# The first 14 slots of a GRU and attention-gated GRU kernel get an order of their own on every engine

## What is computed

```python
def step(h, xp):                       # first recurrence, 50 steps
    hp = h @ Ur + b[1]
    z = sigmoid(xz + hz); r = sigmoid(xr + hr)
    hc = tanh(xh + r * hh)
    return z * h + (1.0 - z) * hc
emb = concatenate([hs, news_b - hs, news_b, hs * news_b], axis=-1)
a = relu(emb @ att_W1 + att_b1); a = relu(a @ att_W2 + att_b2)
ats = sigmoid(a @ att_W3 + att_b3)
def au_step(h, xs):                    # second recurrence, on the first one's states
    u = sigmoid(xu_t + h @ au_Uu); r = sigmoid(xr_t + h @ au_Ur)
    c = tanh(xc_t + r * (h @ au_Uc))
    u_ = at_t * u
    return (1.0 - u_) * h + u_ * c
x = batch_norm(concatenate([h_final, news])); x = leaky(x @ d_W1 + d_b1); x = leaky(x @ d_W2 + d_b2)
y = sigmoid(x @ f_W + f_b)
```

## Time and profile before

| what | value |
|---|---|
| median of 3 runs | 1980.85 us (1979.35 to 1981.06) |
| profiled execution | 1982.23 us, span 1980.4 us |
| PE busy in the span | 1937.3 us, 98% |
| start to R(4) | 36.34 us |
| R(4) to R(14) | 89.20 us |
| R(14) to R(196) | 1737.73 us |
| R(196) to the end | 117 us |

### The profile page before, as it was taken

How to read it: one execution, slowest core, us unless ns; L and a number is a source line. 1 busy time by engine, 2 the same in 40 slices (tenths; PEclk the granted TensorE clock), 3 DMA queues, 4 the chain that set the end, 5 groups by cost and what they waited for, 6 DMA issues and landing times.

```text
span 1980.4 us, 29691 instructions
## 1 busy us (share of the span) xinstructions
PE 1937.3 (98%) x9180; PEld 860.6 (43%) x9180; DVE 1499.0 (76%) x2356; ACT 1452.0 (73%) x2464; POOL 1642.1 (83%) x1396
## 2 busy tenths in 40 slices
PE   6799999999999999999999999999999999999998
PEld 2244444444444444444444444444444444444443
DVE  6677777777777777777777777777777777777775
ACT  5577777777777777777777777777777777777764
POOL 5688888888888888888888888888888888888862
PEclk9899999999999999999999999999999999999999
DMA  3111111111111111111111111111211111111110
GB/s 105 48 54 49 70 50 51 48 69 48 50 70 50 48 64 53 52 49 69 48 48 69 53 48 51 66 48 53 69 48 48 69 48 53 48 69 48 38 44 22
DMA packets 37146, 108.15 MB, mean 55 GB/s; under 512 B 4282, under 2 KB 4538, under 8 KB 30594
## 3 DMA queue, kind: packets, MB, share of 16 engines
q1 hardware_dynamic: 37122, 107.86, 15.4%
HBM read 107.43 MB, written 0.42 MB: 54 GB/s over the span
## 4 chain that ended last, share of the span: by engine, by line
PE 92%; POOL 3%; DVE 2%; issue 1%; ACT 1%; DMA 1%; SPq 0%; DVEq 0%; POOLq 0%; ACTq 0%
PE ps L762 29%; PE ps L763 29%; PE ps L764 29%; PE ps L825 3%; PE ps L816 1%; POOL hn_lo L282 1%; POOL h_lo L288 1%; POOL d L331 1%; DMA score<-score_rows 0%; POOL gus L321 0%; ACT hn_hi L372 0%; DMA x<-in_xs 0%; POOL g_lo L312 0%; POOL x_lo L335 0%; DVE ps L570 0%
## 5 line engine op out<-in xcount | busy, mean ns | idle before, releaser
L762 PE MATMUL ps<-h_hi,w_hi 128*128 128x512 f16 x1384 | 526.5, 380 | 16.2 <-DVE a_lo L650 5.9
L763 PE MATMUL ps<-h_lo,w_hi 128*128 128x512 f16 x1384 | 525.7, 380 | 0.0
L764 PE MATMUL ps<-h_hi,w_lo 128*128 128x512 f16 x1384 | 525.4, 380 | 0.0
L282 POOL TENSOR_TENSOR hn_lo<-hn,hn_hi 128x512 f16<-128x512 f32 x200 | 232.9, 1164 | 187.1 <-ACT hn_hi L372 187.1
L276 POOL TENSOR_TENSOR hn<-h,news 128x512 f32<-128x512 f32 x200 | 256.0, 1280 | 86.5 <-DVE h L668 78.6
L446 ACT ACTIVATE ps<-gt,p_rest 128x512 f32<-128x512 f32 x196 | 135.3, 690 | 216.8 <-DVE gt L665 216.8
L321 POOL TENSOR_TENSOR gus<-gu,score 128x512 f32<-128x512 f32 x200 | 254.8, 1274 | 5.4 <-DMA score<-score_rows 3.8
L331 POOL TENSOR_TENSOR d<-h,hc 128x512 f32<-128x512 f32 x196 | 249.9, 1275 | 6.0 <-ACT hc L474 6.0
L762 PE MATMUL ps<-x_hi,w_hi 128*128 128x512 f16 x599 | 229.3, 383 | 14.4 <-POOL x_lo L335 5.1
L312 POOL TENSOR_TENSOR g_lo<-g,g_hi 128x512 f16<-128x512 f32 x196 | 228.1, 1164 | 17.6 <-ACT g_hi L478 17.6
L656 DVE TENSOR_TENSOR gt<-gr,ps 128x512 f32<-128x512 f32 x196 | 134.9, 688 | 140.3 <-ACT gr L481 140.3
(11 more groups left out here) (123 smaller groups left out, 3706.1 us busy)
## 6 DMA issues: line engine op xcount, KB each, us to landing
x<-in_xs SPq DMA_DIRECT2D x200, 256.0 KB, 3.1
score<-score_rows SPq DMA_DIRECT2D x50, 1024.0 KB, 4.7
news<-in_xs SPq DMA_DIRECT2D x1, 1024.0 KB, 8.5
score_rows<-s_rows SPq DMA_DIRECT2D x50, 8.0 KB
p_rest<-in_pack_rest SPq DMA_DIRECT2D x1, 776.0 KB, 9.3
p_att<-in_pack_att SPq DMA_DIRECT2D x1, 322.0 KB, 6.4
p_gru<-in_pack_gru SPq DMA_DIRECT2D x1, 195.0 KB, 2.6
p_state<-in_pack_state SPq DMA_DIRECT2D x1, 192.0 KB, 8.5
```

Source lines behind the costliest of these rows:

```text
L282: g.tensor_tensor(hn_lo[:, k, :], hn[:, k, :], hn_hi[:, k, :], ALU.subtract).then_inc(hnlo_ready, 1)
L762: m.matmul(ps[:, bank, :], w_hi[:, w, :], hi, start=start, stop=False)
L763: m.matmul(ps[:, bank, :], w_hi[:, w, :], lo, start=False, stop=False)
L764: return m.matmul(ps[:, bank, :], w_lo[:, w, :], hi, start=False, stop=stop)
```

## The change

Slots 4 to 13 get a function `early` of their own on PE, ACT, DVE and POOL, and `slot` is left with slots from EARLY = 14 on. In detail:

- Step 0: R has two banks (B_R and B_A2), so R of item 1 needs no wait and R of item c waits for ACT's r of c - 2. DVE makes t in one instruction. ACT computes 1 - z directly (scale -1 and the bias negated, `b_keep`), so that h is one multiplication. ACT takes the r of item 0 before the fourth x_hi, and DVE two t and one h before the attention weights are prepared.
- Loads: x of item 0 is started from ACT's own queue, ahead of everything on ACT; the state's weights come before the attention's; the candidate news in four parts, `p_rest` after x of step 1.
- Weight splits: state on POOL (after the x_lo of step 0), attention on DVE, gated weights in halves, the hi part on ACT and the lo part on DVE, in slots 8 and 12.
- Slots 4 to 13: the candidate hc goes to PSUM (bank B_GHH, not yet in use), and d = h - hc is made by DVE, not POOL, in place of which e and h take d in place. `attention_1` writes alternately B_GXH and B_A1 for items below 8. The first scores come in slot 8 instead of 9. GXH comes before Z instead of after it.
- Ten matmuls on a zeroed tile come first on PE (`WARM`); their result is not used.
- The batch norm's small instructions go to DVE's slots 196 to 199.

The diff, cut to what the text speaks of:

```diff
-B_Z0, B_XH0 = (B_Z, B_GHH), (B_XH, B_HH)
-B_NEWS = (B_GXH, B_A2, B_GXH, B_XH)
+B_R0, B_Z0, B_XH0 = (B_R, B_A2), (B_Z, B_GHH), (B_XH, B_HH)
+B_NEWS = (B_GXH, B_A1, B_XH, B_A2)
+B_HC = B_GHH
...
+    FIRST_SCORED = SCORED - 1
+    EARLY = LAG + NC
     LOW_DVE = 2
-    AHEAD = 2
+    WARM = 10
+    SPLIT_X, SPLIT_G = LAG - 2, LAG + 2
...
             sp.dma_start(p_gru[:, :], pack_gru).then_inc(gru_landed, 16)
-            for c in range(NC):
-                load_x(0, c).then_inc(x_landed[c], 16)
+            load_x(0, 1).then_inc(x_landed[1], 16)
+            load_x(0, 2).then_inc(x_landed[2], 16)
+            load_x(0, 3).then_inc(x_landed[3], 16)
+            sp.dma_start(p_state[:, :], pack_state).then_inc(state_landed, 16)
             sp.dma_start(p_att[:, :], pack_att).then_inc(att_landed, 16)
-            sp.dma_start(news[:, :, :], xs[T, :, :].rearrange("p (c n) -> p c n", c=NC)).then_inc(news_landed, 16)
-            sp.dma_start(p_state[:, :], pack_state).then_inc(state_landed, 16)
-            sp.dma_start(p_rest[:, :], pack_rest).then_inc(rest_landed, 16)
+            load_news(0)
+            load_news(1)
...
+            g.memset(hn_hi[:, 0, :], 0.0).then_inc(warm, 1)
...
+            def split_state():
+
+                hi = w_hi[:, U_Z:U_Z + 3, :].rearrange("p k m -> p (k m)")
+                lo = w_lo[:, U_Z:U_Z + 3, :].rearrange("p k m -> p (k m)")
+                pool.wait_ge(state_landed, 16)
+                g.tensor_copy(hi, p_state[:, :]).then_inc(state_half, 1)
+                pool.wait_ge(state_half, 1)
+                g.tensor_tensor(lo, p_state[:, :], hi, ALU.subtract).then_inc(state_split, 1)
+
+            def early(low):
+                if low + 2 >= NC:
+                    input_low(low + 2, low + 3)
+                if has(low - LAG - 1):
+                    gated_share(low - LAG - 1, low - LAG, NC)
+                if has(low - 1):
+                    state_news(low - 1, low)
+                    state_low(low - 1, low)
+                    state_news_low(low - 1, low)
+
...
+            a.dma_start(x32[:, 0, :], xs[0, :, 0:CH]).then_inc(x_landed[0], 16)
...
+            first_high(0)
+            first_high(1)
+            first_high(2)
+            act.wait_ge(b_ready, 2)
             reset_first(0)
-            candidate_first(0)
+            first_high(3)
             update_first(0)
             reset_first(1)
-            state_high(0, 1)
+            candidate_first(0)
+            update_first(1)
             reset_first(2)
             candidate_first(1)
+            state_high(0, 1)
+            update_first(2)
+            reset_first(3)
+            candidate_first(2)
+            second_high(0)
             state_news_high(0, 1)
-            update_first(1)
+            state_high(1, 2)
+            update_first(3)
+            candidate_first(3)
             act.wait_ge(att_landed, 16)
             news_part(0)
-            reset_first(3)
-            candidate_first(2)
-            update_first(2)
-            state_high(1, 2)
+            state_high(2, 3)
             state_news_high(1, 2)
             news_part(1)
+            second_high(1)
             relu_1_high(0, 1)
-            candidate_first(3)
-            update_first(3)
             news_part(2)
+            act.wait_ge(a1_pe, 1)
+            state_news_high(2, 3)
+            second_high(2)
...
+                act.wait_ge(t2_ready, low + 1)
+                a.activation(ps[:, B_HC, :], t[:, low % 2, :], ACT.Tanh, bias=b_h).then_inc(hc_ready, 1)
+                act.wait_ge(z_pe, low + 1)
+                a.activation(ps[:, B_Z, :], ps[:, B_Z, :], ACT.Sigmoid, bias=b_zr[:, 0:1]).then_inc(z_ready, 1)
+                if low == NC:
+                    relu_1_high(2, 3)
+                if has(low - LAG - 3):
+                    act.wait_ge(g_ready, low - LAG - 2)
+                    a.activation(g_hi[:, (low - LAG - 3) % NC, :], g32[:, (low - LAG - 3) % NC, :], ACT.Copy).then_inc(ghi_ready, 1)
+                input_high(low + 3, 16 * ((low + 3) // NC + 1), low)
+                if low == SPLIT_X:
+                    split_gated_high(0)
+                if low == SPLIT_G:
+                    split_gated_high(1)
...
-                v.tensor_scalar(t[:, c % 2, :], r[:, c % 2, :], b_hs, None, ALU.mult).then_inc(t1_ready, 1)
-                dve.wait_ge(t1_ready, c + 1)
                 dve.wait_ge(xh_pe, c + 1)
-                v.tensor_tensor(t[:, c % 2, :], t[:, c % 2, :], ps[:, B_XH0[c % 2], :], ALU.add).then_inc(t2_ready, 1)
+                v.scalar_tensor_tensor(out=t[:, c % 2, :], in0=r[:, c % 2, :], scalar=b_hs, in1=ps[:, B_XH0[c % 2], :],
+                                       op0=ALU.mult, op1=ALU.add).then_inc(t2_ready, 1)
 
             def new_state_first(c):
 
                 dve.wait_ge(hc_ready, c + 1)
                 dve.wait_ge(z_ready, c + 1)
-                v.tensor_tensor(ps[:, B_Z0[c % 2], :], hc[:, c % 2, :], ps[:, B_Z0[c % 2], :], ALU.mult).then_inc(e_ready, 1)
-                dve.wait_ge(e_ready, c + 1)
-                v.tensor_tensor(h32[:, c, :], hc[:, c % 2, :], ps[:, B_Z0[c % 2], :], ALU.subtract).then_inc(h_ready, 1)
+                v.tensor_tensor(h32[:, c, :], hc[:, c % 2, :], ps[:, B_Z0[c % 2], :], ALU.mult).then_inc(h_ready, 1)
...
+            def early(low):
+                k = low % 2
+                if pairs_of(low - 1):
+                    low_2(0, paired(low - 1))
+                dve.wait_ge(hh_pe, low - NC + 1)
+                dve.wait_ge(r_ready, low + 1)
+                v.scalar_tensor_tensor(out=t[:, k, :], in0=ps[:, B_HH, :], scalar=b_hs,
+                                       in1=r[:, k, :], op0=ALU.add, op1=ALU.mult).then_inc(t1_ready, NC + 1 if low == NC else 1)
+                if has(low - LAG - 1):
+                    gated_difference(low - LAG - 1, low - LAG)
+                dve.wait_ge(c_ready, min(low - 1, NC))
+                item = low - 2 if low > NC else 1
+                attention_1_news(item, item + 1)
+                if pairs_of(low - 1):
+                    low_2(1, paired(low - 1))
+                dve.wait_ge(t1_ready, low + 1)
+                dve.wait_ge(xh_pe, low + 1)
+                v.tensor_tensor(t[:, k, :], t[:, k, :], ps[:, B_XH, :], ALU.add).then_inc(t2_ready, 1)
+                if has(low - LAG - 1):
+                    gated_step(low - LAG - 1, low - LAG)
+                attention_1_low(item, item + 1)
+                if has(low - LAG - 1):
+                    gated_state(low - LAG - 1, low - LAG)
+                dve.wait_ge(hc_ready, low + 1)
+                v.tensor_tensor(d[:, k, :], h32[:, low % NC, :], ps[:, B_HC, :], ALU.subtract).then_inc(d_early, 1)
+                dve.wait_ge(d_early, low - NC + 1)
+                dve.wait_ge(z_ready, low + 1)
+                v.tensor_tensor(d[:, k, :], d[:, k, :], ps[:, B_Z, :], ALU.mult).then_inc(e_ready, NC + 1 if low == NC else 1)
+                dve.wait_ge(e_ready, low + 1)
+                v.tensor_tensor(h32[:, low % NC, :], d[:, k, :], ps[:, B_HC, :], ALU.add).then_inc(h_ready, 1)
+                if low == NC:
+                    dve.wait_ge(c_ready, 3)
+                    attention_1_news(2, 3)
+                    attention_1_low(2, 3)
+                if low == SPLIT_X:
+                    split_gated_low(0)
+                if low == SPLIT_G:
+                    split_gated_low(1)
...
+                if s == LOOP_HI:
+                    dve.wait_ge(rest_landed, 16)
+                    bn_guess()
+                    bn_newton(0)
+                if s == LOOP_HI + 1:
+                    bn_newton(1)
+                    bn_newton(2)
+                if s == LOOP_HI + 2:
+                    bn_newton(3)
+                    bn_fold()
+                if s == LOOP_HI + 3:
+                    bn_news()
...
+            pe.wait_ge(warm, 1)
+            for _ in range(WARM):
+                m.matmul(ps[:, B_A1, :], hn_hi[:, 0, 0:P], hn_hi[:, 0, :], start=True, stop=True)
...
+                    if c >= 2:
+                        pe.wait_ge(r_ready, c - 1)
+                    split_product(B_R0[c % 2], W_R, *x, start=True, stop=True).then_inc(r_pe, 1)
...
+                news_part(c)
+            pe.wait_ge(att_split, 1)
+            pe.wait_ge(c_ready, 1)
+            attention_1(0, 1)
+            pe.wait_ge(state_split, 1)
+            pe.wait_ge(t2_ready, NC)
+            candidate_state(0, 1)
...
+            def early(low):
+                x = (x_hi[:, low % NC, :], x_lo[:, low % NC, :])
+                h = (h_hi[:, (low - NC) % HIST, :], h_lo[:, (low - NC) % HIST, :])
+                hg = (h_hi[:, (low - LAG) % HIST, :], h_lo[:, (low - LAG) % HIST, :])
+
+                pe.wait_ge(r_ready, low)
+                if score_of(low - 1):
+                    pe.wait_ge(s_ready, scored(low - 1))
+                pe.wait_ge(xlo_ready, low + 1)
+                split_product(B_R, W_R, *x, start=True, stop=False)
```

(49 more changed lines are left out.)

354 lines of the change are left out of this document (192 added, 162 removed).

## The result

The changed kernel takes 1973.73 us (median of 7 runs, 1971.77 to 1976.53), the kernel before 1980.85 (7 runs, 1979.35 to 1982.16): ratio 0.9964, 95% interval 0.9952 to 0.9975. It is faster by 7 us where 19 were forecast, and at 1973.73 us it lies 1.7 us above the range of 8 in 10 (1950 to 1972). Its profiled execution took 1972.17 us with a span of 1970.3.

What follows compares the result with a forecast made beforehand. PE bounds the kernel, busy 98% of the span; R(14) to R(196) stays 1737.73 us. A gain of 21.8 us ahead of R(14), less 3 at the end, makes -18.8: 1962.0 us, 8-in-10 range 1950 to 1972.

Steps and rivals of the forecast that it cites:

- Start to R(4): Kernel start to first matmul of slot 4's R product: 36.3 us becomes 23.4.
- the two held instructions: In step 0, two waits where DVE and POOL hold each other up, charged 2.4 us.
- The warm-up's gift: Ten warm-up matmuls cost nothing; what they give the first products is hidden by ACT's r.
- R(4) to R(6): Slots 4 and 5, between starts of their R products: 16.8 us becomes 15.0.
- POOL now sets the pace: Up to R(6), each item costs POOL four instructions, 4.6 us; hn_lo of item 3 ends at 33.8.
- R(6) to R(10): Slots 6 to 9: 36.4 us becomes 24.0, PE setting the pace at 5.2 us a slot, with d on DVE.
- rival 3: Slots 6 to 9: POOL stays pacemaker at 7.5 us a slot (+9), time 1972; 1968 to 1976, chance 0.19.
- R(9)'s wait: Slot 9's R product waits 1.6 us for the score's sigmoid, behind other work on ACT.
- R(11) to R(14): Slots 11 to 13: GXH ahead of Z waits 2.8 us for g; 18.6 us to R(13), then 13.2.
- The clock, +3: Slots 11 to 13: clock falls behind two of three waits, 1.5 us each; between 0 and 6.
- The end, +3: After R(196): batch norm in slots 196 to 199 costs 3.5 us a slot, less slack; 3 of 0 to 7.
- rival 2: Slots 196-199: all 27 batch-norm instructions wait for POOL, 28.0 us, time 1987; 0.06 with anything beyond 1977, half at full price.

Runs made afterwards that it cites:

- run 3: Changed kernel with one DVE instruction moved: c_news of item 2 in slot 4 ahead of a_lo of item 1; 1973.0 us, ratio 0.9955.
- run 10: Two kernels: changed kernel without its ten warm-up matmuls, 1977.23 us; changed kernel with first input again on SP's queue behind p_gru, 1976.09 us.
- run 7: Changed kernel with GXH behind Z (slots 11-13), c_news of item 2 earlier, 22 small batch-norm instructions singly in slots 14-35, large one in 196; 1957.88 us.
- run 9: Changed kernel with d = h - candidate on POOL again in slots 4 to 13 and the candidate in SBUF; 1982.09 us, ratio 1.0007.
- run 1: Changed kernel with the GXH product of slots 11 to 13 behind Z again; 1967.85 us, ratio 0.994.
- run 2: Changed kernel with ten useless matmuls on PE ahead of the wait for g in slots 11 to 13; 1972.38 us, ratio 0.9958.
- e_spread: Changed kernel with GXH behind Z, c_news of item 2 earlier, batch norm spread over step 0 and slots 14, 196, 198, 200; 1965.41 us, ratio 0.9917.
- e_bn_late: Changed kernel with its batch-norm instructions moved from slots 196-199 to slots 200 and 201; 1973.51 us, ratio 0.9969.
- run 5: Changed kernel with the batch-norm instructions back in early slots, where the kernel before has them; 1981.67 us, ratio 1.0.

## Why the prediction was right or wrong

The span was to be 1961.6 and is 1970.3. The 8.7 us are 5.9 ahead of R(14) and 2.9 in the end; the median lies another 1.6 above the profiled execution.

**Start to R(4), 23.4 against 24.27: right in the number**, with errors in it that cancel. r of item 0 starts at 7.26 for 8.2 and h of item 0 at 10.52 for 12.1; the two held instructions cost 1.9 us for the 2.4 charged. Without a fall of the clock step 0 is 22.8 (run 3); the fall costs 1.5. The warm-up's gift was put at nothing, as hidden by ACT's r; it is 2 us (run 10). R(4) also matters less than the sum takes it to: R(6) doesn't follow it (run 3).

**R(4) to R(6), 15.0 against 18.89: the step that failed.** I had "POOL now sets the pace" and ran its instructions back to back to R(6). They are so up to hn_lo of item 3, which starts at 31.48 us. Then POOL stood 3.64 us for x_hi(7), behind an ACT that stood for a DVE instruction placed behind h. I had walked the queue of one engine and not the other two. In place of POOL's pace PE had two waits that the sum lacks, 1.88 us for t and 2.06 for a_lo(3), and about 1.2 us of a fall. Run 3 moves the instruction: the wait for t goes, the other falls to 1.6, and R(6) is at 39.8. The last 1.5 us to the forecast 38.4 stay also in run 7; there too POOL stands for x_hi(7), 1.25 us, and PE 1.63 us for a_lo(3).

**R(6) to R(10), 24.0 against 26.09: PE sets the pace, as forecast.** Slots 6 and 7 take 5.67 and 5.18 us, and rival 3 had 7.5. That the time itself falls in rival 3's interval, 1968 to 1976, is chance. But the reason that I gave, d on DVE, isn't what makes these two slots 5.2: run 9 has d on POOL, and the same slots but for a fall in slot 6. Mis-sized is R(9)'s wait, 2.66 for 1.6; z, x_hi and the gated split stand ahead of the sigmoid on ACT, as I had written, and take longer than I counted. The rest is the tail of a clock fall in slot 6 (0.5 us) and odd parts.

**R(11) to R(14): right.** The wait for g was put at 2.8 and is 2.93, 2.94 and 3.25; 9.58 and 13.16 us against 9.3 and 13.2. I took it as the price of the change and did not say that it could be left out. It could: run 1.

**The clock, +3: near in its sum, by luck.** Up to R(14) this execution shows three falls, at 17 to 22, 40.9 to 44 and 92.4 to 95.3 us, of 1.5 to 1.8 each. I charged two behind the waits for g, and these had one of the three. The first is ahead of R(4) and doesn't reach R(6), so 3.2 us count. What a fall costs was right (1.5). Run 2 ties the falls in slots 11 to 13 to PE's idle time.

**The end, +3 against +5.9: mechanism right, size off.** Two held instructions to a series, 3.4 to 3.6 us against 3.5 priced. The mis-sized term is the slack that was to take them in, 0.5 to 1.5 us a slot. The first series costs nothing (R(197) is on time), the second 1.4, the third 0.9, and the rest appears behind R(199): 3.6. The slack was counted anew for each slot, and the lateness adds up instead. A likely reason, which no run isolates, is that DVE idles where it waits for ACT and POOL, and these are late for the same reason. I also miscounted: 22 small instructions, not 26, which leaves the price of a series as it is and rival 2 too dear. Rival 2 is refuted, as POOL does run dry.

The rule of the Trainium skill ("SBUF — State Buffer", section "Who interferes with whom") that two such instructions lock each other out whole agrees with the rows of the tail and of step 0 here: 1.07 to 1.27 us of an instruction of 0.16 while POOL had work, and 0.16 as soon as it had none.

**What stays open.** Of waits of the same length some are followed by a fall and some not, in the same code (2.91 us at 16.5 in the changed kernel's execution was followed by one, 2.91 us at 16.6 in e_spread's was not). What decides that no run shows. It is also the likely reason why the changed kernel's runs spread over 4.8 us where those of the kernel before spread over 2.8. The mean granted clock of each run speaks for it: 0.994 in the slowest of the changed kernel's seven, 1976.53 us, and 0.997 in the other six; in e_bn_late 0.994 in the two slowest (1975.91 and 1974.51) and 0.997 in the two fastest (1971.14 and 1971.79). But only one execution of each kernel has a trace, so where the others lost it isn't shown. Open too are the last 1.5 us at R(6), and what took slots 6 and 7 to 5.2 us, as it wasn't d alone.

## What to carry to other kernels

When an order is written out by hand for several engines, walk each engine's queue for each slot and ask of every instruction who stands behind its wait. Two of the losses here were one DVE instruction three places too late (some 2 us, and one wrong step of the forecast), and one product ahead of another (5 to 6 us). Small VectorE instructions beside a busy GpSimd are to be counted by the GpSimd instructions that start meanwhile, not by their own time, and go best singly, right behind the result that releases GpSimd. An early stretch that shortens also loses its cover: the batch norm's 23 instructions stood in early slots of 8 to 10 us before, and in slots of 5 they cost 15 us (run 5), half of it through the clock. And where PE's waits of 2 us and more are followed by falls, a price at the full clock is too low: add the clock to each rival.

## What the runs showed of the hardware

- Of a series of small DVE instructions behind h in a steady slot, the first takes 0.16 us, the second and third 1.25 and 1.19, the rest 0.16. Placed singly at the same place, 22 of 22 took 0.15 to 0.16. With six POOL instructions in a row, six were held, each for 1.07 to 1.26.
- Behind waits of 2.0 to 4.5 us the granted clock fell to the lower level (0.42 us a matmul), mostly for 1.3 to 1.8 us a fall (7 to 9 matmuls of 128x512 outside attention_2), in some executions behind one such wait, in others behind another. The longest cost 2.6 to 2.9 us (runs 3, 5, 6, 9 and 10). Behind waits of 1.04 to 1.33 (run 1, three of them) it did not fall; in the kernel before it fell behind one of 1.51, at 94.24 us, for nine matmuls:

```profile
94.24 0.59 PE L762 MATMUL ps<-x_hi,w_hi 128*128 128x512 f16 x1 [1.51 <-ACT gu L463]
94.62 0.63 PE L763 MATMUL ps<-x_lo,w_hi 128*128 128x512 f16 x1
```

- A load on a second queue, started with the first one's, made p_gru land 4.2 us after its issue, for 2.5 with all loads on one queue, and still r of item 0 starts 1.1 us earlier with it (7.26 for 8.40).
